# Drains for VectorE's own waits and hand-offs in fours in a graph network kernel

## What is computed

```python
# L0: edge convolution
e   = relu((x[dst] - x[src]) @ theta_w.T + theta_b + x[src] @ phi_w.T + phi_b)
x   = layernorm(x + segment_max(e, dst))        # 0 where a node has no edge
# L1: message passing, two rounds, then a read-out
hv  = x @ W_in + b_in
for W, b in ((W_u0, b_u0), (W_u1, b_u1)):
    m  = relu(concat(hv[src], he) @ W + b)
    hv = where(has_in, segment_max(m, dst) + hv, hv)
y   = relu(hv @ W_ro + b_ro)
out = layernorm(x + y)
```

## Time and profile before

| | us |
|---|---|
| median of 3 runs | 3338.57 (3336.08 to 3339.93) |
| span of the profiled execution, first to last instruction | 3822.6 |
| GpSimd busy | 2418.9 (63%) |
| TensorE busy | 2221.9 (58%) |
| VectorE busy | 1446.2 (38%) |
| ScalarE busy | 187.7 (5%) |
| DMA, mean share of 16 engines and rate | 201 GB/s |
| mean granted TensorE clock | 0.781 |

### The profile page before, as it was taken

The page is one execution under the profiler, slowest core; times in us unless marked ns, Lnnn a source line. Parts: engine busy times, 40 slices in busy tenths (PEclk is TensorE's granted clock), DMA queues, the critical chain, the costliest instruction groups (busy, mean ns, idle before and its releaser), DMA issues.

```text
span 3822.6 us, 20106 instructions
## 1 busy us (share of the span) xinstructions
PE 2221.9 (58%) x5442; PEld 1094.0 (29%) x5442; DVE 1446.2 (38%) x3430; ACT 187.7 (5%) x422; POOL 2418.9 (63%) x2536
## 2 busy tenths in 40 slices
PE   5121211112223657777777777775787878877776
PEld 4111111111112423333333333352333333333335
DVE  2345454345544423333333333321333333333336
ACT  1000000000001400000000000010000000000004
POOL 4577666677665366666666666456666666666644
PEclk7565555555556978899898888887888889889888
DMA  7366666566554456666666656565666666666654
GB/s 248 108 209 206 207 207 196 184 203 213 196 193 166 151 167 208 219 210 219 212 224 205 225 195 221 191 207 166 216 228 213 225 218 221 224 216 219 218 176 127
DMA packets 265646, 769.90 MB, mean 201 GB/s; under 512 B 55443, under 2 KB 114686, under 8 KB 227902
## 3 DMA queue, kind: packets, MB, share of 16 engines
q0 software_dynamic: 122208, 334.92, 29.0%
q1 hardware_dynamic: 84478, 354.64, 24.2%
q10 hardware_dynamic: 58848, 79.06, 6.8%
HBM read 421.22 MB, written 347.19 MB: 201 GB/s over the span
## 4 chain that ended last, share of the span: by engine, by line
PE 41%; DVE 23%; another core or an unknown queue 21%; issue 9%; DMA 2%; ACT 1%; POOL 1%; DVEq 1%; ACTq 0%; POOLq 0%
DVE hist L372 18%; PE edge_ps L757 17%; PE edge_ps L754 16%; PE edge_ps L698 3%; PE side_ps L698 3%; DVE junk L305 1%; DVE junk L302 1%; POOL gath L538 1%; DVEq L370 1%; ACT x_sb L649 1%; PE side_ps L767 1%; DMA gath<-table,src_sb 0%; DVE above L286 0%; ACT gath L649 0%
## 5 line engine op out<-in xcount | busy, mean ns | idle before, releaser
L538 POOL DMA_INDIRECT gath<-table,src_sb x2352 | 2256.0, 959 | 1166.8 <-issue 631.3
L372 DVE SCALAR_TENSOR_TENSOR hist<-hist,lift,edge_ps 128x256 f32<-128x256 f32 x1568 | 753.6, 481 | 1537.4 <-PE edge_ps L757 670.3
L754 PE MATMUL edge_ps<-w_e,he_sb 128*128 128x512 f32 x1568 | 927.3, 676 | 530.1 <-DVE hist L372 406.3
L757 PE MATMUL edge_ps<-gath,ident 128*128 128x512 f32 x1568 | 894.2, 655 | 16.4 <-DMA gath<-table,src_sb 14.8
L706 PE MATMUL side_ps<-dst_f,onehot 128*128 128x512 f32 x200 | 147.3, 891 | 815.5 <-DVE onehot L288 720.4
L754 PEld LDWEIGHTS edge_ps<-w_e,he_sb 128*128 128x128 f32 x1568 | 303.3, 210 | 992.6 <-issue 568.5
L372 DVE SCALAR_TENSOR_TENSOR hist<-hist,lift,gath 128x256 f32<-128x256 f32 x784 | 380.7, 486 | 369.9 <-DVE hist L372 127.0
L757 PEld LDWEIGHTS edge_ps<-gath,ident 128*128 128x128 f32 x1568 | 331.2, 212 | 457.1 <-issue 436.5
L706 PEld LDWEIGHTS side_ps<-dst_f,onehot 128*128 128x128 f32 x200 | 58.0, 320 | 893.3 <-DVE onehot L288 742.7
L608 ACT COPY hv_sb<-side_ps 128x256 f32<-128x256 f32 x147 | 54.7, 372 | 3332.7 <-remote 1031.9
L565 POOL DMA_INDIRECT gath<-runs,end_row x147 | 142.8, 972 | 92.9 <-issue 38.1
(11 more groups left out here) (119 smaller groups left out, 972.1 us busy)
## 6 DMA issues: line engine op xcount, KB each, us to landing
runs<-hist SPq DMA_DIRECT2D x294, 1024.0 KB
he_sb<-in_he ACTq DMA_DIRECT2D x196, 256.0 KB
gath<-table,src_sb POOLq DMA_INDIRECT x2352
table<-hist SPq DMA_DIRECT2D x72, 256.0 KB
back_T<-x1T ACTq DMA_DIRECT2D x98, 128.0 KB
back_T<-in_xT ACTq DMA_DIRECT2D x49, 128.0 KB
x_sb<-in_x SPq DMA_DIRECT2D x49, 128.0 KB
back_T<-msgT ACTq DMA_DIRECT2D x49, 128.0 KB
```

The lines of the kernel that those rows point to most:

```text
L372: V.scalar_tensor_tensor(hist[:, s % H, :], hist[:, (s - 1) % H, :], lift[:, t:t + 1], edges, ALU.add, ALU.max).then_inc(state_done, 1)
L538: pool.indirect_dma_start(gath[:, s % G, :], None, tables[r], bass.IndirectOffsetOnAxis(src_sb[:, t:t + 1], 0)).then_inc(gathered[s % G // ...
L754: T.matmul(bank, he_sb[:, c % NHE, at:at + P], w_e[r - 1][:, :], start=True, stop=False)
L757: T.matmul(bank, ident[:, :], flat(gath[:, at:at + 2, :]), start=False, stop=True).then_inc(pair_summed, 1)
```

## The change

VectorE's waits for its own instructions become drains (`V.drain()`), in the setup, in `pick_rows` and `find_ends`, in `edge_maxima` (one in front of every maximum) and in `norm_units` (three a unit); the semaphores that only served this go. `query` counts two a turn. `state_done` is raised at each fourth maximum, and TensorE's `pair_summed` becomes `group_summed`, raised after two pairs; VectorE, GpSimd and ScalarE wait for groups of four steps. GpSimd's waits stand in every fourth step. The edge sums have six PSUM banks; the four banks of the transposes are the last two of these and two of their own, and the query, join and node products move with them.

```diff
+GS = 4
+GROUPS = STEPS // GS
+EDGE_BANKS = 6
-QSTEPS = 10
...
+        edge_ps = ctx.enter_context(nc.psum_tensor("edge_ps", [P, EDGE_BANKS, 2 * D], f32))
+        side_ps = ctx.enter_context(nc.psum_tensor("side_ps", [P, 2, 2 * D], f32))
+        wide = lambda u: (unit(u)[1] - unit(u)[0]) * D
+        product_ps = lambda u: edge_ps[:, u % BANKS, 0:wide(u)]
+        turned_ps = lambda u: edge_ps[:, BANKS + u % 4, 0:wide(u)] if u % 4 < 2 else side_ps[:, u % 4 - 2, 0:wide(u)]
+        query_ps = edge_ps[:, BANKS:BANKS + 2, :].rearrange("p b f -> p (b f)")
+        back_ps = side_ps[:, 0, 0:D]
+        join_ps = [edge_ps[:, BANKS + n, 0:D] for n in range(2)]
...
+            def pick_rows(along):
+                V.drain()
+                V.tensor_scalar(above[:, :], along, bounds[:, 0:1], None, ALU.is_ge)
+                V.drain()
...
             def edge_maxima(r):
...
-                    if s % 2 == 0 and r == 0:
+                    if r == 0 and s % 2 == 0:
                         dve.wait_ge(gathered[s % G // 2], 2 * 16 * (s // G + 1))
-                    elif s % 2 == 0:
-                        dve.wait_ge(pair_summed, s // 2 - PAIRS + 1)
-                    if s > 0:
-                        dve.wait_ge(state_done, s)
-                    edges = gath[:, s % G, :] if r == 0 else edge_ps[:, (s // 2) % BANKS, (s % 2) * D:(s % 2 + 1) * D]
-                    V.scalar_tensor_tensor(hist[:, s % H, :], hist[:, (s - 1) % H, :], lift[:, t:t + 1], edges,
-                                           ALU.add, ALU.max).then_inc(state_done, 1)
+                    elif r > 0 and s % GS == 0:
+                        dve.wait_ge(group_summed, s // GS - GROUPS + 1)
+                    V.drain()
+                    bank, half = s // 2 % EDGE_BANKS, s % 2 * D
+                    edges = gath[:, s % G, :] if r == 0 else edge_ps[:, bank, half:half + D]
+                    state = V.scalar_tensor_tensor(hist[:, s % H, :], hist[:, (s - 1) % H, :], lift[:, t:t + 1], edges,
+                                                   ALU.add, ALU.max)
+                    if s % GS == GS - 1:
+                        state.then_inc(state_done, 1)
...
             def norm_units(n, to_sum, add):
...
-                        add(u, y).then_inc(summed, 1)
+                        added = add(u, y)
+                        if n == 1:
+                            added.then_inc(summed, 1)
                     if u > 0:
                         dve.wait_ge(std_ready, m)
-                        V.reciprocal(rstd[:, before, :], std[:, before, :]).then_inc(rstd_ready, 1)
+                        V.reciprocal(rstd[:, before, :], std[:, before, :])
+                    V.drain()
                     if u < NU:
-                        dve.wait_ge(summed, m + 1)
-                        V.scalar_tensor_tensor(y, y, 0.0, flat(x_sb[:, lo:hi, :]), ALU.max, ALU.add).then_inc(resid_added, 1)
+                        V.scalar_tensor_tensor(y, y, 0.0, flat(x_sb[:, lo:hi, :]), ALU.max, ALU.add)
                     if u > 0:
-                        dve.wait_ge(rstd_ready, m)
                         V.scalar_tensor_tensor(shift[:, before, :], mv[:, before, :, 0], -1.0, rstd[:, before, :],
                                                ALU.mult, ALU.mult).then_inc(shift_ready, 1)
                     if u < NU:
-                        dve.wait_ge(resid_added, m + 1)
+                        V.drain()
                         for k in range(hi - lo):
-                            V.bn_stats(stats[:, at, k, :], to_sum(u)[:, k, :]).then_inc(stats_made, 1)
+                            V.bn_stats(stats[:, at, k, :], to_sum(u)[:, k, :])
+                        V.drain()
                         for k in range(hi - lo):
-                            dve.wait_ge(stats_made, n * TILES + lo + k + 1)
                             last = V.bn_aggr(mv[:, at, k, :], stats[:, at, k, :])
...
             def gather_edges(r):
...
-                    if s % 2 == 0 and G <= s < STEPS + G:
-                        pool.wait_ge(state_done, s - G + 2)
-                    elif s % 2 == 0 and s >= G:
-                        pool.wait_ge(pair_summed, (s - G) // 2 - PAIRS + 1)
+                    if s % GS == 0 and G <= s < STEPS + G:
+                        pool.wait_ge(state_done, (s - G) // GS + 1)
+                    elif s % GS == 0 and s >= G:
+                        pool.wait_ge(group_summed, (s - G) // GS - GROUPS + 1)
...
             def messages(r):
+                for g in range(GROUPS):
+                    n = (r - 1) * GROUPS + g
+                    c = n * GS // HC
+                    if n * GS % HC == 0:
+                        pe.wait_ge(he_loaded[c % NHE], 16 * (c // NHE + 1))
+                    if g * GS >= 2 * EDGE_BANKS:
+                        pe.wait_ge(state_done, r * GROUPS + g - 2 * EDGE_BANKS // GS + 1)
+                    for k in range(0, GS, 2):
+                        s = r * STEPS + g * GS + k
+                        bank = edge_ps[:, s // 2 % EDGE_BANKS, :]
+                        at = s % HC // 2 * P
+                        T.matmul(bank, he_sb[:, c % NHE, at:at + P], w_e[r - 1][:, :], start=True, stop=False)
+                        pe.wait_ge(gathered[s % G // 2], 2 * 16 * (s // G + 1))
+                        last = T.matmul(bank, ident[:, :], flat(gath[:, s % G:s % G + 2, :]), start=False, stop=True)
+                    last.then_inc(group_summed, 1)
```

More of the change, by code:

```diff
@@ L236, in _, with reached @@
         def _(dve):
-            done = [0]
             V = nc.vector
-            def after():
-                dve.wait_ge(setup_step, done[0])
-            def step(ins):
+            after = V.drain
+            def reached(name, ins):
                 ins.then_inc(setup_step, 1)
-                done[0] += 1
+                setup_at[name] = len(setup_at) + 1
             V.memset(next_i[:, :], FAR).then_inc(cleared, 1)
@@ L249, in _ @@
             V.memset(w_e[1][:, :], 0.0).then_inc(cleared, 1)
-            step(V.memset(none_row, LOWEST))
-            setup_at["none row"] = done[0]
+            reached("none row", V.memset(none_row, LOWEST))
             dve.wait_ge(conv_loaded, 16 * len(conv_loads))
[L253 to L256, removed]
@@ L276, in _ @@
             after()
[L277 to L280, removed]
+            V.memset(bounds[0:1, 0:1], 0.0)
+            V.tensor_scalar(lift[:, :], lift[:, :], 1.0, -LOWEST, ALU.subtract, ALU.mult)
+            V.tensor_scalar(joins_lift[:, :], joins_lift[:, :], 1.0, -LOWEST, ALU.subtract, ALU.mult)
@@ L281, in _ @@
+            V.tensor_copy(node_no[:, :], part_no[:, :])
             after()
-            def pick_rows(q, along):
-                if q > 0:
-                    dve.wait_ge(query, QSTEPS * q)
-                V.tensor_scalar(above[:, :], along, bounds[:, 0:1], None, ALU.is_ge).then_inc(query, 1)
-                dve.wait_ge(query, QSTEPS * q + 1)
+            def pick_rows(along):
+                V.drain()
+                V.tensor_scalar(above[:, :], along, bounds[:, 0:1], None, ALU.is_ge)
+                V.drain()
@@ new lines, in find_ends @@
+                V.drain()
+                V.tensor_tensor(found[:, 0:1], counts[:, 0:1], counts[:, 1:2], ALU.is_gt)
+                V.tensor_scalar(found[:, 1:2], counts[:, 2:3], float(NONE), None, ALU.subtract)
+                V.drain()
+                V.tensor_scalar(at, found[:, 1:2], found[:, 0:1], float(NONE), ALU.mult, ALU.add)
+                V.tensor_scalar(bounds[:, :], bounds[:, :], by, None, ALU.subtract)
+                V.tensor_scalar(node_no[:, :], node_no[:, :], by, None, ALU.add).then_inc(query, 1)
@@ L324, in _ @@
+            V.tensor_tensor(at_end[:, 2:3], dst_f[:, STEPS - 1:STEPS], next_f[:, 1:2], ALU.not_equal)
+            V.tensor_scalar(at_end[:, 3:4], part_no[:, :], float(SPARE), None, ALU.add)
             after()
-            step(V.scalar_tensor_tensor(fix_to[:, :], at_end[:, 0:1], at_end[:, 2:3], at_end[:, 3:4], ALU.mult, ALU.add))
-            setup_at["rows to fix"] = done[0]
+            V.tensor_tensor(at_end[:, 0:1], at_end[:, 0:1], at_end[:, 3:4], ALU.subtract)
+            after()
+            reached("rows to fix", V.scalar_tensor_tensor(fix_to[:, :], at_end[:, 0:1], at_end[:, 2:3], at_end[:, 3:4],
+                                                          ALU.mult, ALU.add))
@@ L330, in bias_columns @@
                 for h in range(KH):
[L331 to L332 removed]
+                    last = V.tensor_copy(b_in_cols[:, h, :], b_in_col[:, h:h + 1].to_broadcast([P, P]))
+                reached("b_in columns", last)
             def weights_and_biases():
```

148 lines of the change are left out of this document (56 added, 92 removed).

## The result

The changed kernel takes 3348.91 us (3348.29 to 3349.81, 5 runs), the kernel before in the same comparison 3336.08 us (3332.34 to 3339.93, 5 runs): ratio 1.0041, interval 1.0029 to 1.0053. It is slower by 13 us, clear of the scatter of the runs. The forecast was 3343 and no measurable change, with 0.23 for slower. The measured time lies in the 80% range (3275 to 3360), but above the forecast's own 3335 to 3345. By its number it is nearer to B (3353) than to the forecast; B's mechanism is not what happened, as the experiments show.

The account below looks back on a forecast made before the run. GpSimd's gathers, 1.25 us each, were taken to pace the runs. From the median of 3338.6, +2 for hand-offs in fours and +3 for the last phase gave 3343 us; own range 3335 to 3345, 80% range 3275 to 3360.

Parts of the forecast that it names:

- B: Rival, slower: drains in the last phase's loop let VectorE's own work pass the loop; 3353 us, chance 0.23.
- The lateness is nearly all the profiled execution's own: Late signals in the edge rounds, 377 us of excess in the profile, were taken to be nearly absent from the runs.
- the 76 us that the sum left over: Profiled span less edge stalls, 3415 us, still 76 above the median; 60 of it read as gathers 24 ns shorter in runs.
- Drains in the maxima: Edge maxima on VectorE: drains replace 2352 semaphore waits of 0.055 us, hidden behind the gathers even at 0.30 each; 0 us.
- The last sentence of the prediction: Wrong altogether if the free gather pace itself changed, say by VectorE's drains in round 0 lengthening the 0.987 us.
- Hand-offs in fours: Ends of rounds 1 and 2: one more pair of maxima, 1.0 us each, before the store and fix-up; +2 us.
- Ring and banks: Edge rounds: the ring of gathered steps covers 2.5 us less but isn't full; TensorE doesn't wait for banks; 0 each.
- The last phase: Closed loop of 2.71 us a unit: the residual now waits for the reciprocal, 0.12 a unit over 25 units; +3 us.
- The rule weighed there: Last phase: the pipeline empties after each operation anyhow, so count operations, not semaphores; this term 0, the sum 3341 us.
- The profile's span: The profiled execution was expected to get 100 to 350 us shorter, as the late signals are fewer.
- Rival A: Faster: late signals are in the runs too, with a gather pace below 1.226 us, and the change recovers them; 3280 us, chance 0.36.
- C: Rival: the change does nothing, tails hide behind stores and drains are free; 3339 us, sharing 0.41 with the forecast.

Follow-up runs that it names:

- both_waits: The changed kernel with self waits by semaphore again in the maxima and the layer norms' unit loop; 3337.50 us, 1.0015 of the kernel before.
- after_b: The changed kernel, unaltered, run again beside the kernel before in a job with late signals; 3843.39 us, 1.0041 of the kernel before.

## Why the prediction came out as it did

**What bounds the kernel**: right. GpSimd's gathers at 1.25 us pace the runs; rounds 1 and 2 take 784 x 1.25 in both kernels.

**"The lateness is nearly all the profiled execution's own"**: wrong. The late signals were the job's. In every later job the profiled execution and the plain runs agree, at some 3333 or at 3830 to 3870 us. So a profiled execution is not by itself longer than a run, and the first trace (3822.6) and the first times (3338.57) are of different conditions, most likely of different jobs, which isn't on record. The conclusion drawn from it, that the runs have no stall left, was right for the times at hand. The gather pace in the runs was not 24 ns shorter, though: the 76 us that the sum left over were row phases and ends that the late signals stretched too, beyond the 31 taken off for them (the last phase from its first reciprocal 87.2 in that trace, 68.7 free).

**Drains in the maxima, "Hidden at either end: 0"**: this step failed. VectorE's own time was hidden, as said (spacing 0.559 for 0.520). What I left out is that VectorE's maxima lengthen gathers that start just after them, and the gathers are the path: their longer duration in round 0 was in the rows, and I kept it fixed at 0.987. Round 0's gathers measured +8.4 us, of which both_waits, without the drains in the maxima, gives back 5.8; the rest is not divided. The price of a meeting is shown, the reason for the larger number is not. The last sentence of the prediction names the place, as something that would make it wrong.

**Hand-offs in fours, +2**: the mechanism was right for rounds 1 and 2; the size was +2.4 and +2.0 instead of +1.0 each, of which 1.2 each are the maxima that were forecast and the rest TensorE's later hand-over. Ring and banks cost nothing in mid-round, as said.

**The last phase, +3**: right in mechanism, short in size. 0.12 a unit was taken, 0.19 measured in the steady units (2.70 to 2.89), +4.6 in the phase and 1 more before its first reciprocal, which was not divided. The drain's own cost, 0.07, lay between the ends, nearer the low one. B's condition, VectorE's own work passing the loop at 0.09 a drain, was not reached.

The rule weighed there (the Trainium skill, "VectorE: DVE Perf Modes", "The DRAIN you can't avoid") has the pipeline emptied after each operation anyhow, but the same section says that a next operation that isn't held starts earlier, which the prediction left out: L405's start within L402 is no disagreement with it. Its rule is on semaphores and says nothing of a drain instruction. Here an explicit drain cost 0.039 us more a maximum than the semaphore it replaced (0.559 against 0.520) and 0.16 us where no wait was binding (0.24 against 0.08). So the explicit drain is not free, and a term of 0 by that rule would have been too low.

**The profile's span, shorter by 100 to 350 us, "as the late signals are fewer"**: wrong. It fell by 475 since its job had none; where they were, it did not fall.

**Rival A**: the gather pace is 1.250 where it needed less than 1.226, and in a job where late signals are in the runs the change gains nothing (after_b). **C**: refuted, the loss is clear of the scatter and the last phase shows its drains.

In all, the forecast was +5 us and the loss is 13. The time fell into a range that was made wide, to 3360, for dear drains in the last phase; the greatest single part of the loss, in round 0, was put at nothing. That the range held is in part luck.

## What to carry to other kernels

Replace a semaphore wait by a drain only after asking what the semaphore didn't hold up: the drain holds everything behind it, and in a closed loop over several engines that adds up unit by unit. When one engine's instruction is the pace of a whole phase, an engine with slack beside it isn't free either: compare that instruction's mean duration (here 0.960 and 0.971 us), not only its idle time. Before a trace is used with a set of times, check that its span fits them; if it doesn't, get a trace from the same job.

## What was not expected of the hardware

The same kernel ran at 3333 us in one job and at 3854 us in another on the same chip, with the gather pace of 1.25 us unchanged in free stretches, and the difference in signals that arrive late. It moved the ratio of two kernels little (1.0041 in both conditions), though not from the same places: with late signals round 0's gathers last longer in the kernel before (0.989 us against 0.975), without them in the changed one (0.960 against 0.971).

GpSimd's indirect gather (0.946 us) is lengthened when one of VectorE's maxima with both inputs in SBUF starts 0.10 to 0.34 us before it: by 0.21 us on average at 0.1 to 0.2, by 0.10 at 0.2 to 0.3, so that it ends 1.30 us after the maximum's start; at other distances by about 0.01 us or less on average. When the maxima read one input from PSUM, in rounds 1 and 2, the gathers keep 0.946 us. The Trainium skill, "GPSIMD Engine Reference", section "Specifications", names contention with VectorE operations that have two SBUF inputs, and gives no size; the sizes here are of these traces.
